# Scatters that wait later, and the sort's sums of x in two float32r parts in place of three bf16 parts

## The reference

```
src_h = h[src] @ W_msg.T + b_msg
msg = src_h + emb
messages = jax.ops.segment_sum(msg, dst, num_segments=num_nodes)
h_new = _gru_cell(messages, h[:num_nodes], W_ih, W_hh, b_ih, b_hh)
...
ee = ea @ enc_w + enc_b
src = x[ei[1]]
h = jnp.concatenate([src, ee], axis=1) if concat else src + ee
agg = jax.ops.segment_sum(h, ei[0], num_segments=x.shape[0])
h = agg @ w1 + b1
h = jax.nn.relu(_bn_eval(h, g, be, rm, rv))
return h @ w2 + b2
```

## Time and profile before

| what | before |
|---|---|
| timed runs (3), median, lowest to highest | 6228.43 us, 6224.02 to 6235.12 us |
| profiled execution, span from first to last instruction | 6981.5 us |
| mean granted TensorE clock, profiled execution | 0.859 |
| TensorE, VectorE, ScalarE, GpSimd busy | 77%, 54%, 47%, 60% |

### The profile page before, as it was taken

The page is one execution under the profiler, slowest core; times in us unless marked ns, Lnnn a source line. Parts: engine busy times, 40 slices in busy tenths (PEclk is TensorE's granted clock), DMA queues, the critical chain, the costliest instruction groups (busy, mean ns, idle before and its releaser), DMA issues.

```text
span 6981.5 us, 88118 instructions
## 1 busy us (share of the span) xinstructions
PE 5386.3 (77%) x26429; PEld 3361.9 (48%) x26429; DVE 3769.9 (54%) x14165; ACT 3302.5 (47%) x4432; POOL 4213.9 (60%) x4243
## 2 busy tenths in 40 slices
PE   4376767676766764666676999999898998898998
PEld 1133333333333322333344666666666666666666
DVE  8576767777766754455566444443333333444443
ACT  1164545555655641122122666665555554554554
POOL 5655555555555556666631666666676666666665
PEclk5588988888988985677776999999999999999999
DMA  7165556556655652333323666667666667666665
GB/s 250 48 144 129 140 121 138 127 134 136 157 127 127 148 138 76 98 101 102 100 78 121 188 190 185 194 196 220 184 186 179 190 191 217 184 184 174 177 185 148
DMA packets 1068177, 1066.40 MB, mean 153 GB/s; under 512 B 494051, under 2 KB 784501, under 8 KB 1067701
## 3 DMA queue, kind: packets, MB, share of 16 engines
q1 hardware_dynamic: 889573, 782.05, 40.1%
q0 software_dynamic: 178128, 278.65, 16.0%
HBM read 747.21 MB, written 216.68 MB: 138 GB/s over the span
## 4 chain that ended last, share of the span: by engine, by line
PE 44%; another core or an unknown queue 6%; DVE 4%; issue 4%; ACT 2%; DMA 1%; SPq 0%; DVEq 0%; ACTq 0%
PE ps L2965 27%; PE ps L2935 4%; PE ps L2848 2%; PE ps L2899 2%; PE ps L2809 2%; PE ps L2810 1%; DVE BIG L2197 1%; PE ps L2909 1%; PE ps L2910 1%; PE ps L2811 1%; ACT MSR L2575 1%; DVE MSR L2258 0%; PE ps L2812 0%; PE ps L2914 0%
## 5 line engine op out<-in xcount | busy, mean ns | idle before, releaser
L3051 POOL DMA_INDIRECT GL<-h_gathered,IDXA x2058 | 2112.6, 1027 | 1227.7 <-issue 568.5
L2965 PE MATMUL ps<-MSR,HP 128*128 128x512 f32 (+1 forms) x9000 | 2375.0, 410 | 174.9 <-ACT MSR L2575 71.2
L3017 POOL DMA_INDIRECT rec_q<-BIG x1563 | 1513.7, 968 | 1156.2 <-issue 473.6
L2575 ACT CAST MSR<-MS 128x1024 fp32r<-128x1024 uint8 (+1 forms) x1500 | 1491.8, 1028 | 1272.9 <-PE ps L2965 820.3
L2965 PEld LDWEIGHTS ps<-MSR,HP 128*128 128x128 f32 x9000 | 1675.6, 195 | 624.9 <-issue 168.5
L2750 PE MATMUL ps<-MTB,XPS 128*128 128x512 bf16 x4410 | 1312.2, 416 | 1.1 <-DMA XPS<-x_parts 0.8
L2258 DVE CAST MSR<-MS 128x1024 fp32r<-128x1024 uint8 (+1 forms) x750 | 522.6, 699 | 1236.7 <-PE ps L2965 738.5
L2457 ACT CAST MT<-ps 128x512 uint16<-128x512 f32 x735 | 427.4, 582 | 959.2 <-remote 633.3
L2461 ACT CAST MTB<-MT 128x1024 bf16<-128x1024 uint8 x735 | 767.9, 1045 | 64.8 <-PE ps L2750 10.3
L3033 POOL DMA_INDIRECT BIG<-x_parts,SRCq x611 | 582.8, 954 | 341.5 <-issue 164.4
L2750 PEld LDWEIGHTS ps<-MTB,XPS 128*128 128x128 bf16 x4410 | 439.7, 103 | 248.7 <-issue 68.1
(11 more groups left out here) (248 smaller groups left out, 6244.4 us busy)
## 6 DMA issues: line engine op xcount, KB each, us to landing
MS<-counts SPq DMA_DIRECT2D x1080, 256.0 KB
counts<-BIG SPq DMA_DIRECT2D x360, 256.0 KB
XPS<-x_parts SPq DMA_DIRECT2D x192, 384.0 KB
GL<-h_gathered,IDXA POOLq DMA_INDIRECT x2058
rec_q<-BIG POOLq DMA_INDIRECT x1563
rec_q<-BIG SPq DMA_DIRECT2D x44, 490.0 KB, 10.4
HTI<-h_cols SPq DMA_DIRECT2D x72, 256.0 KB
h_dense<-PCL SPq DMA_DIRECT2D x30, 512.0 KB
```

The costliest lines, as they stand in the source:

```text
L2575: s.copy(MSR[:, g % RM, :, 0:w].rearrange("p t (c s) -> p t c s", s=P), MSB[:, i % MR, 0:4 * w].rearrange("p (c h s t) -> p h t c s", h=2, ...
L2965: got = t.matmul(bank[:, 0:w], HP[:, d, part, :], MSR[:, g % RM, d % 2, 0:w], start=d + part == 0, stop=lay > 0 and d + part == BD, skip_g ...
L3017: g.indirect_dma_start(out=RAd, out_offset=bass.IndirectOffsetOnAxis(ap=POSI[:, c:c + 1], axis=0), in_=RECA[q % 3][:, c - a, :], in_offset ...
L3051: g.indirect_dma_start(out=GL[:, r % LR, i, 0:3 * P], out_offset=None, in_=HGd[lay], in_offset=bass.IndirectOffsetOnAxis(ap=IDXA[:, a + i: ...
```

## The change

In the scatter loop the wait moves from the second tile of a four to the first, and is for the four before the last one. For the sums, x is split into two float32r parts (a rounded copy and the rest) beside the three bf16 parts, which the gathers still read; the two parts have a DRAM array of their own, and one more store in each step. The widened counts are written as float32r, so that buffers grow, and several others (`Y`, `PC`, `XMT`, `RT`, `RZ`, `DD`) now share their memory: ScalarE waits before the first widening until all parts are stored, and VectorE waits for the last sum before it prepares the weights.

```
+        XRd = nc.dram_tensor("x_parts_wide", (NP, 2 * P), F32).ap()
...
+        MTB = sb("MTB", [P, 3, 2048], F32R, cells)
+        XPS = sb("XPS", [P, 3, 4, 2, P], F32R, cells)
...
-        MTB = sb("MTB", [P, 3, 2048], BF16, front)
-        XPS = sb("XPS", [P, 3, 4, 3, P], BF16, front)
...
 def x_rest(v, i):
+            v.tensor_tensor(XR[:, i % 2, 0:n, 1, :], Y[:, i % 2, 0:n, :], XR[:, i % 2, 0:n, 0, :].bitcast(F32), ALU.subtract)
             v.tensor_tensor(RT[:, 0:n, :], Y[:, i % 2, 0:n, :], PC[:, i % 2, 0:n, 0, :], ALU.subtract).then_inc(*rest1.inc())
...
 def weights_vector(v):
             v.wait_ge(w_in.sem, 192)
+            v.wait_ge(xd.sem, len(CELLS))
...
 def cells_scalar(s, m):
+                if i == 0 and m == 0:
+                    for k in range(2):
+                        s.wait_ge(xp_out[k].sem, 2 * stored(SG - 1 - k))
...
 def x_high(s, i):
-                s.wait_ge(xp_out[i % 2].sem, 16 * (i // 2))
+                s.wait_ge(xp_out[i % 2].sem, 32 * (i // 2))
+            s.copy(XR[:, i % 2, 0:n, 0, :], Y[:, i % 2, 0:n, :])
             s.copy(PC[:, i % 2, 0:n, 0, :], Y[:, i % 2, 0:n, :]).then_inc(*part1.inc())
...
 def sums_tensor(t, c):
-            for part in range(3):
+            for part in range(2):
...
 def quick_gpsimd(g):
-                    if quad and (c - a) % GT == 1:
-                        g.wait_ge(scat[q % 3][(quad - 1) % 2].sem, scattered_to(q, quad - 1))
+                    if quad >= 2 and (c - a) % GT == 0:
+                        g.wait_ge(scat[q % 3][quad % 2].sem, scattered_to(q, quad - 2))
...
 def blocks_sync(y, k):
-            y.dma_start(XPS[:, k % 3, 0:n, :, :].rearrange("p b a f -> p b (a f)"),
-                        XPd[512 * u:512 * u + P * n, :].rearrange("(b p) f -> p b f", p=P)).then_inc(*xps_in[k % 3].inc(16))
+            y.dma_start(XPS[:, k % 3, 0:n, :, :].rearrange("p b a f -> p b (a f)").bitcast(F32),
+                        XRd[512 * u:512 * u + P * n, :].rearrange("(b p) f -> p b f", p=P)).then_inc(*xps_in[k % 3].inc(16))
...
 def x_out_sync(y, i):
+            y.dma_start(XRd[512 * i:512 * i + P * n, :].rearrange("(b p) f -> p b f", p=P),
+                        XRW[:, i % 2, 0:256 * n].rearrange("p (b f) -> p b f", f=2 * P)).then_inc(*xp_out[i % 2].inc(16))
```

More of the change, by code:

```diff
@@ L1633, in program @@
         IO256 = sb("IO256", [P, 256], F16, front)
-        XMT = sb("XMT", [P, 2, 2 * P], F32, front)
-        Y = sb("Y", [P, 2, 4, P], F32, front)
-        PCW = sb("PC", [P, 2, 1024], F32, front)
+        cells = ExitStack()
+        MTB = sb("MTB", [P, 3, 2048], F32R, cells)
+        XPS = sb("XPS", [P, 3, 4, 2, P], F32R, cells)
+        cells.close()
+        MTBW = sb("MTBW", [P, 3 * 2048], F32, front)
+        XPSW = sb("XPSW", [P, 3 * 4 * 2 * P], F32, front)
+        Y = MTBW[:, 0:1024].rearrange("p (q b f) -> p q b f", q=2, b=4)
+        PCW = MTBW[:, 1024:3072].rearrange("p (q c) -> p q c", q=2)
+        XRW = MTBW[:, 3072:5120].rearrange("p (q c) -> p q c", q=2)
+        XR = XRW.bitcast(F32R).rearrange("p q (b a f) -> p q b a f", b=4, a=2)
+        XMT = XPSW[:, 2560:3072].rearrange("p (q c) -> p q c", q=2)
+        RT = XPSW[:, 2048:2560].rearrange("p (b f) -> p b f", b=4)
         PC = PCW[:, :, 0:768].bitcast(BF16).rearrange("p q (b a f) -> p q b a f", b=4, a=3)
@@ L1639, in program @@
         TY0 = sb("TY0", [P, 4, 9], F32, front)
-        TAS = PCW[:, :, 768:836].rearrange("p q (c k) -> p q c k", k=17)
-        RT = sb("RT", [P, 4, P], F32, front)
+        TAS = sb("TAS", [P, 2, 4, 17], F32, front)
         XT = sb("XT", [P, 2, 512], F32, front)
         MT = sb("MT", [P, 3, 1024], BF16, front)
-        MTB = sb("MTB", [P, 3, 2048], BF16, front)
-        RZ = MTB[:, 2, 0:1024].bitcast(F32).rearrange("p (a b) -> p a b", a=2)
-        DD = MTB[:, 2, 1024:2048].bitcast(F32).rearrange("p (a b) -> p a b", a=2)
-        XPS = sb("XPS", [P, 3, 4, 3, P], BF16, front)
+        RZ = MTBW[:, 3072:3584].rearrange("p (a b) -> p a b", a=2)
+        DD = MTBW[:, 3584:4096].rearrange("p (a b) -> p a b", a=2)
         IOTM = sb("IOTM", [P, 7, NB // 7 + 2], F16, front)
@@ L1651, in program @@
         front.close()
-        recx0 = XPS[:, :, :, :, :].rearrange("p q b a f -> p (q b a f)").bitcast(F32)
+        recx0 = XPSW
         RECX = [recx0[:, IX * RW * i:IX * RW * (i + 1)].rearrange("p (c w) -> p c w", w=RW) for i in range(2)]
@@ L2748, in sums_tensor @@
                 t.wait_ge(acc_out.sem, x.j - 1)
-            for part in range(3):
+            for part in range(2):
                 got = t.matmul(PS[6 + x.j % 2][:, :], XPS[:, x.load % 3, i, part, :], MTB[:, m % 3, 512 * i:512 * (i + 1)],
-                               start=4 * x.u + i + part == 0, stop=4 * x.u + i + part == NB + 1)
+                               start=4 * x.u + i + part == 0, stop=4 * x.u + i + part == NB)
             got.then_inc(*xd.inc())
@@ L3026, in quick_gpsimd @@
             for i in range(2):
-                g.wait_ge(xp_out[i].sem, stored(SG - 1 - i) + 16 * (i == 0))
+                g.wait_ge(xp_out[i].sem, 2 * stored(SG - 1 - i) + 16 * (i == 0))
             for q in range(QS0, NQ0):
@@ L3081, in blocks_sync @@
                 for i in range(2):
-                    y.wait_ge(xp_out[i].sem, stored(SG - 1 - i))
+                    y.wait_ge(xp_out[i].sem, 2 * stored(SG - 1 - i))
             if k >= 3:
```

## The result

The changed kernel takes **5889.83 us** (median of 4 runs, 5886.33 to 5900.0) against 6230.41 us before (4 runs, 6224.02 to 6235.12): ratio 0.9453, 95% interval 0.9431 to 0.9475. It is 340 us faster. The forecast was 6070 us, 160 us faster, with a range down to 5965: the direction was right, the size was less than half of the measured one.

A forecast was written before the change was run, and what follows sets the result against it. The sort was read as bound by the scatter stream (2271 us), VectorE's path (2130) close behind. Scatter wait 141 plus sums 15 made 156 us, so 6228 became 6072, say 6070 us; range 5965 to 6240.

The forecast's parts named there:

- the scatter wait's term: In the sort, moving the scatters' wait removes 261 us of landing waits until VectorE is late next: worth 141 us.
- The stream's length, 2271 us: GpSimd's scatter stream in the sort without waits for VectorE: start, busy time, issue and 261 us of landing waits.
- The second way to the same number: Sort's end at 2675 us less 426 us, its proportional share of late-signal time missing from timed runs: 2249 us.
- What is late next, 2130 us: VectorE's path through the sort without late TensorE signals, claimed to bound it once the scatters' landing waits go.
- The landing itself: A scatter's landing takes at most some 6.2 us, so no wait of over 1.1 us remains after the change.
- The sums of x: TensorE's 1470 cells: two float32r products for three bf16, 384 us less busy, mostly hidden; gain 15 us, bounds 0 to 110.
- The blocks of x: 200 loads of 512 KB for 384 KB, 25 MB more in the sort: costs nothing.
- The steps on x: 25 steps before 190 us gain a copy, a subtraction and a store: taken at 0, between -36 and +35 us.
- New waits and the rest: ScalarE's wait before widening and VectorE's before preparing weights cost nothing, the latter under the last scatters; nothing changes after the sort.
- B: Rival, chance 0.14: faster products also free VectorE, closing its 110 us of gaps in the sort: 5977 us.
- C: Rival, chance 0.18: late signals are in the timed runs too, VectorE's path sets the sort, gain hidden: about 6225 us.
- D: Rival, chance 0.12: less TensorE work makes gaps in the sort, its clock falls and the kernel gets slower: 6292 us.

The follow-up runs named there:

- the wait alone: The kernel before with only the new scatter wait, sums of x staying three bf16 products: 5875.63 us, ratio 0.9416.
- the wait with double stores: The kernel before with the new scatter wait and each of the 25 stores of the x parts made twice: 5876.92 us, ratio 0.942.
- second profile of before: The kernel before, unchanged, profiled once more: 6241.9 us in one run, span 6239.3.
- the wait over eights: The kernel before with the new wait counted in eights, for the eight before the last; sums stay three bf16 products: 5861.54 us, ratio 0.9399.

## Why the prediction was wrong, point by point

**The step that failed is the scatter wait's term**, "2271 - 2130 = 141": it measured 368 us. Both of its ends were wrong.

*The stream's length, 2271 us.* It was put together from 261 us of landing waits. That profile was of an execution with late TensorE signals. I saw that, and took VectorE's lateness off; but a scatter that starts late finds the four before it landed, so the same lateness had also *hidden* landing waits. The rows fit that: 139 landing waits in that profile, 229 undisturbed. Undisturbed they are 415.6 us, and the scatters end at 2405.5. The stream cannot be had from a disturbed trace by leaving one kind of wait out: the waits trade with each other. The second way to the same number, 2675 - 426 = 2249, gave the late signals to the sort in proportion to the waits for them. In fact the sort had lost 269 of the 742 us between the two spans. That the two ways met was chance, and I counted it as evidence.

*What is late next, 2130 us.* It took VectorE's 1753 us from 320 on, among them 110 us of other gaps, and started it from an opening in which scatters and VectorE were both late. Undisturbed, VectorE is done at about 1967 us with the wait alone and waits 77.5 us for the last scatters. Without the landing waits that are left, the stream there would still end near 2011 us (2041.8 - 30.8, an estimate). So VectorE's path did not cap the gain at 141 us; one scatter's delay of the wait alone gave 243.

*A missed follower.* I wrote that behind this wait on GpSimd stand only later scatters. That holds for GpSimd's queue; ScalarE's record step waits for the window three before as well, and through it TensorE and VectorE. In the disturbed trace this wait hardly shows (31.2 us, once); undisturbed it is 294.9 us in the stretch, and 27.6 with the new wait. VectorE's 244.8 us of waits behind TensorE and ScalarE went with it, to 20.6.

*The landing itself* was read a little short: at most 1.1 us was to be left with four scatters in between; the longest wait left in the wait alone is 2.6 us. The undisturbed longest wait of 6.3 us in place of 4.9 gives 2.5 by the prediction's own working. The sum, 30.8 us, is under the 40 that were forecast. The Trainium skill ("DMA: Bandwidth & Descriptors", Rules for kernel authors) advises to wait on a transfer's semaphore late, so that its fixed cost lies under other work. The runs agree: the first 1.26 us of lateness, from the second scatter of a four to the third, was worth 243 us, and the remaining 2.5 us together another 116.

*The sums of x*, taken at a gain of 15 us (bounds 0 to 110): for the products themselves this holds. Two in place of three gave 23 us with the old wait and 6 us, not to be told from none, with the new one. Their relief of TensorE was oversized, 384 us from a line of the disturbed profile: undisturbed, the three products take 1198.0 us (the wait with double stores) and the float32r ones 990.3, 208 us less. What missed is the float32r form as a whole, which the sum had at +15 with all that comes with it at nothing: 50 us slower without the wait, 14 to 23 us slower with it. The Trainium skill ("FP8 and Floating Point Precision", TensorE Precision Notes) says that true FP32 takes four passes through the array. That rule did not bear on the float32r products: 990.3 us for 2940 is 0.34 us each, where a bf16 product of the same shape took 0.31 (904.0 us for 2940, two bf16 products with the new wait).

*The blocks of x*, costed at nothing because TensorE does not wait for them. It does not (2.7 us after). But their bytes go over the same 16 DMA engines as the scatters: with the old wait, full blocks cost 70 us (64 by the ratios) and 47 us of landing waits. I asked who waits for the added transfer, and not whose transfer it delays. The Trainium skill ("DMA: Bandwidth & Descriptors", SWDGE vs HWDGE vs iDMA) says that each DMA engine goes round between its queues for both kinds of issue, GpSimd's and SP's. The rows fit that; they do not show the turn by turn.

*The steps on x*, taken at 0 between -36 and +35 us: against the wait alone some 18 us by the counts of scatters, inside the bounds.

*New waits and the rest:* VectorE's new wait shows as 4.8 us under the last scatters, as costed. Nothing changed behind the sort: 3833.8 us from the last scatter's start to the span's end in the second profile of before, 3835.1 in the changed one.

*The rivals.* B's time, 5977, was the nearest, by a mechanism that the runs refute. C rested on the late signals being in the timed runs; they are not. (Its sum, 6228 + 17 - 15, is 6230 and not 6225; nothing hangs on it.) D's clock went the other way as a whole, and the experiments take it apart. From 320 to 1900 us the granted clock, between its levels of 1.2 and 2.4 GHz, was 0.89 in the second profile of before and 0.97 with the wait alone, where TensorE is busy 1371 of 1580 us in place of 1176. With two bf16 products in place of three it fell, as D had it, to 0.86 with the old wait and to 0.93 with the new one; but neither of these two kernels got slower for it. The Trainium skill ("TensorE: Matmul & The Clock Gate", A second HAM failure mode) tells of a clock that goes back and forth, at a loss of throughput, when TensorE idles briefly between groups of matmuls. The lower clocks with fewer products agree with that; no loss of time shows here.

*With the undisturbed rows* the sum would have been 6244 less (415.6 - 30.8 = 384.8), plus 22.5 us more of waits for VectorE (22.2 to 44.7), 5882 us, for the wait alone: measured 5875.6. As 30.8 and 44.7 come from that run itself, this shows that the stream's terms add up, and is no forecast.

## What to carry to other kernels

When a profiled span is far above the timed median, don't subtract the waits that look foreign: take a second profile of the same kernel first, for the other waits in it may have changed too. A wait for a landing on the queue that bounds a stage costs nearly its whole length each time: here 385 us of landing waits went and the time fell by 368. Three more scatters between issue and wait were worth far more than TensorE's relief, and the next deeper wait was worth little. And for every byte added, ask whose landing it delays, not only who waits for it.

## What the runs showed of the hardware

Two profiles of one kernel differed by 742 us (6981.5 and 6239.3), spread over all stages, with the semaphores of matmuls arriving late in one alone; the timed median was 6228.43. Why the signals came late in that one, no run shows. The granted clock of the first 320 us was 1.00 in some profiled executions and 0.52 to 0.57 in others, with no effect on the time that shows: the kernel with the lowest median, the wait over eights, had 0.57 there, and took 5865.71 us in that execution and 5859.38 to 5864.67 us in its others.
